# A transformer block and a linear attention block: the ramp in front of the loop re-dealt over ScalarE and VectorE

## The reference, cut to what matters

```
# block 0, for each sequence
mod = c @ ada_w.T + ada_b                     # six parts: shift, scale, gate, twice
h   = rmsnorm(x) * (1 + sc_msa) + sh_msa
q, k, v = h @ qkv_w.T                         # 16 heads of 8
q, k = rmsnorm(q), rmsnorm(k)                 # over the 8 of a head
q, k = rope3d(q, k, positions)                # sin and cos of the positions
o   = softmax(q k^T / sqrt(8)) v
x   = x + g_msa * (o @ proj_w.T + proj_b)
x   = x + g_mlp * ((silu(h2 @ w1.T) * (h2 @ w3.T)) @ w2.T)    # h2: the modulated norm of x
# block 1: layer norm, linear attention with softmax of q over 8 and of k over the tokens,
# modulated norm, silu, output projection
out = x + c * h
```

## Time and profile before

| | us |
|---|---|
| median of 3 runs | 212.56 (212.43 to 212.91) |
| the profiled execution's own time | 211.97 |
| its span, first to last instruction | 210.2 |

### The profile page before, as it was taken

How to read it: one execution, slowest core, us unless ns; L and a number is a source line. 1 busy time by engine, 2 the same in 40 slices (tenths; PEclk the granted TensorE clock), 3 DMA queues, 4 the chain that set the end, 5 groups by cost and what they waited for, 6 DMA issues and landing times.

```text
span 210.2 us, 5867 instructions
## 1 busy us (share of the span) xinstructions
PE 183.4 (87%) x1986; PEld 141.1 (67%) x1986; DVE 164.0 (78%) x488; ACT 130.7 (62%) x354; POOL 135.9 (65%) x346
## 2 busy tenths in 40 slices
PE   1796868889999999899999999999998799998742
PEld 1544556667777777777776787788886478887522
DVE  4798898897979799996666434778899589999851
ACT  1476696677777777676555784453432367999740
POOL 8889798989786867758800783167512546757642
PEclk9999999999999999999999999999999999999995
DMA  5963000000000000000000000000000000001102
GB/s 111 280 178 142 0 5 3 0 0 3 3 3 2 3 6 0 3 3 2 3 3 0 3 3 0 2 0 0 6 0 0 0 2 3 0 25 30 51 26 74
DMA packets 9915, 5.13 MB, mean 24 GB/s; under 512 B 3025, under 2 KB 9758, under 8 KB 9758
## 3 DMA queue, kind: packets, MB, share of 16 engines
q1 hardware_dynamic: 6494, 4.08, 6.4%
q10 hardware_dynamic: 3392, 0.68, 1.6%
HBM read 3.71 MB, written 1.05 MB: 23 GB/s over the span
## 4 chain that ended last, share of the span: by engine, by line
PE 61%; DVE 21%; ACT 6%; issue 6%; POOL 2%; ACTq 2%; POOLq 0%; DVEq 0%
PE bank L1769 8%; DVE qkpad L1500 8%; PE bank L1778 7%; PE bank L1860 6%; PE bank L799 5%; PE bank L810 5%; PE bank L800 5%; PE bank L786 4%; PE bank L920 3%; PE bank L1801 2%; PE bank L1837 2%; PE bank L1872 2%; PE bank L852 2%; ACT probs L1201 2%; PE bank L1830 2%
## 5 line engine op out<-in xcount | busy, mean ns | idle before, releaser
L1201 ACT ACTIVATE probs<-bank 128x512 f32<-128x512 f32 x64 | 34.7, 594 | 22.6 <-PE bank L1778 22.5
L1500 DVE TENSOR_REDUCE qkpad<-bank 128x4 f32<-128x512 f32 x64 | 41.0, 684 | 9.1 <-PE bank L1769 7.7
L1778 PE MATMUL bank<-qTm,kBD 32*128 32x128 f32 x512 | 37.1, 283 | 0.4 <-ACT probs L1201 0.4
L1769 PE MATMUL bank<-kBD,qTs 32*128 32x256 f32 x224 | 31.7, 399 | 5.7 <-DVE qkpad L1500 4.2
L1778 PEld LDWEIGHTS bank<-qTm,kBD 32*128 32x128 f32 x512 | 31.0, 186 | 1.0 <-ACT probs L1201 0.6
L1769 PEld LDWEIGHTS bank<-kBD,qTs 32*128 32x128 f32 x224 | 19.8, 184 | 10.8 <-DVE qkpad L1500 7.4
L545 ACT ACTIVATE th<-bank 128x256 f32<-128x256 f32 x24 | 9.2, 384 | 18.9 <-PE bank L800 15.5
L1860 PE MATMUL bank<-probs,vpad 128*32 128x128 f32 x512 | 18.5, 277 | 0.2
L1051 POOL TENSOR_TENSOR partner<-qk,rope 128x96 f32<-128x96 f32 x32 | 14.3, 467 | 6.7 <-ACT qk L1243 6.7
L1801 PE MATMUL bank<-ident,qkpad 128*128 128x128 f32 x96 | 16.5, 281 | 0.8 <-DVE qkpad L1598 0.8
L481 POOL TENSOR_SCALAR var<-mv 128x2 f32<-128x2 f32 x16 | 3.1, 193 | 20.3 <-DVE mv L672 18.4
(11 more groups left out here) (250 smaller groups left out, 512.3 us busy)
## 6 DMA issues: line engine op xcount, KB each, us to landing
gate<-in_cond_dram SPq DMA_DIRECT2D x1, 1024.0 KB, 4.6
out_dram<-res SPq DMA_DIRECT2D x8, 128.0 KB, 1.8
xin<-in_x_dram ACTq DMA_DIRECT2D x2, 256.0 KB, 5.1
xin<-in_x_dram SPq DMA_DIRECT2D x1, 512.0 KB, 4.9
ada_n<-in_L_cond_ada_w_dram SPq DMA_DIRECT2D x1, 256.0 KB, 5.2
w_n<-in_L_cond_w_dram SPq DMA_DIRECT2D x2, 128.0 KB
qkv_n<-in_L_cond_qkv_w_dram SPq DMA_DIRECT2D x1, 192.0 KB, 3.9
w_n<-in_L_cond_w_dram SPq DMA_DIRECT2D x1, 170.5 KB
```

What stands on the lines that cost most here:

```text
L1201: q.activation(probs[2 * r + i][:, :, :, :].rearrange("p f a t -> p (f a t)"), bank[E_BANK[i]][:, :], ACT.Exp, scale=SCALE).then_inc(s_p, 1)
L1500: q.tensor_reduce(out_, score_bank(b, r, i)[:, :].rearrange("p (f a t) -> p f a t", f=2, a=2), X_AXIS, ALU.max, negate=True).then_inc(s_ma ...
L1769: last = q.matmul(bank[S_BANK[i]][:, f * 2 * T:(f + 1) * 2 * T], qTs[b % 2][rows, f, :], kBD[b % NKB][rows, f, :, :].rearrange("p a t -> p ...
L1778: last = q.matmul(bank[E_BANK[i]][:, (2 * f + k) * T:(2 * f + k + 1) * T], kBD[t % NKB][rows, f, k, :], qTm[t % 2][rows, f, :], start=True ...
```

## The change

The head of the work is dealt anew; what is computed stays the same.

- A constant tile `warm` of 128 x 512 bf16 ones is set by VectorE as its first instruction. TensorE computes products of it, into banks that are overwritten later, in eight places of the ramp: 5, 2, 2, 1, 6, 3, 4 and 3 of them in front of waits.
- The load of sequences 4 to 7 moves from ScalarE's DMA queue to SyncE's, and the load of the rest of `ada_w` ahead of the load of sequences 8 to 15.
- The copy of the first part of `adaT` goes from VectorE to ScalarE. The squares of sequence 0 come in front of the sine.
- The sums of squares of sequences 4 to 7 are made by ScalarE with its accumulator, four rows of squares, and GpSimd adds the small constant; those of sequences 8 to 11 and 12 to 15 are made in loop steps 0 and 1, between the modulation and the second round's exponentials, and GpSimd takes the powers for four sequences at a time.
- The masks and one of the eight value tiles are set by VectorE at its start.
- Sequence 0: VectorE splits the keys and ScalarE the queries (`first_queries`), out of another bank. Sequence 2 is split by ScalarE instead of VectorE.
- The reciprocal root of sequences 4 and 5 is refined by VectorE, in seven steps right in front of the loop, instead of by GpSimd in step 0.
- On ScalarE `silu_input` comes directly behind the queries of sequence 0, and the split of sequence 1 in front of the copy of w1, the evictions of sequence 4 and the modulation of sequence 5. On TensorE the product of sequence 4 and the turning of input 5 come behind the early scores.
- Of the five small modulations behind step 0 two stay there (`V_GATE1`) and three go behind step 4.

```diff
@@ SyncE and ScalarE DMA queues
+            sp.dma_start(xin[:, HEAD_B:MID_B, :], x[HEAD_B:MID_B, :, :]...).then_inc(ld_mid, 16)
+            sp.dma_start(ada_n[:, 2:6, :], ...).then_inc(ld_ada, 16)
             sp.dma_start(xin[:, MID_B:, :], ...).then_inc(ld_x, 16)
-            sp.dma_start(ada_n[:, 2:6, :], ...).then_inc(ld_ada, 16)
...
-            input_rows(slice(HEAD_B, MID_B), ld_mid)
@@ GpSimd
+            def input_spread(rows, ready, k):
+                g.wait_ge(pv_a, ready)
+                q.tensor_scalar(ms[:, rows], ms[:, rows], 1.0, EPS0, ALU.mult, ALU.add).then_inc(p_ms, 1)
+                g.wait_ge(p_ms, k)
...
-                if not is_seq(b) or b % 2 == 0:
+                if not is_seq(b) or b % 2 == 0 or b // 2 in BY_VECTOR:      # BY_VECTOR = (0, 2)
...
-            input_rstd(slice(HEAD_B, MID_B), V_MSMID)
             turned_partner(1)
             turned_own(1)
+            input_spread(slice(HEAD_B, MID_B), A_MID, 1)
+            input_rstd(slice(HEAD_B, MID_B))
             added(1)
@@ ScalarE
             q.activation(big[:, 0:HEAD_B, :], xin[:, 0:HEAD_B, :], ACT.Square).then_inc(pv_a, 1)
+            a.wait_ge(pt, P_ADA1)
+            q.activation(adaT[:, 0:2 * D], bank[1][:, 0:2 * D], ACT.Copy).then_inc(pv_a, 1)
...
+            def square_sums_of_rows(first, sm):
+                a.wait_ge(sm, 16)
+                for b in range(first, first + HEAD_B):
                     q.activation(big[:, b, :], xin[:, b, :], ACT.Square, scale=D ** -0.5, accum_out=ms[:, b:b + 1]).then_inc(pv_a, 1)
...
+            def first_queries():
+                a.wait_ge(s_tq, 1)
+                a.wait_ge(masked, 2)
+                q.activation(qTs[0]..., bank[S_BANK[0]][:, 0:2 * T], ACT.Identity, scale=rowmask[:, 0:1]).then_inc(h_q, 1)
...
             modulated_input(1)
-            input_squares(slice(HEAD_B, MID_B), ld_mid)
+            squares(0)
             angles()
-            squares(0)
...
             input_normed(5)
+            first_queries()
+            silu_input()
             modulated_input(4)
+            keys_and_queries(1)
             weights(P_W1, ...)
             squares(4)
             queries_keys(4)
             values(4)
             modulated_input(5)
-            keys_and_queries(1)
             weights(P_W3, ...)
...
-            silu_input()
             queries_and_max(0)
+            keys_and_queries(2)
...
-            square_sums_of_rows()
...
                 modulated_input(t + 6)
+                if t < 2:
+                    square_sums_of_rows(MID_B + HEAD_B * t, ld_x)
                 exp(t, 1, 0)
@@ VectorE
+            q.memset(warm[:, :], 1.0).then_inc(warmed, 1)
             keys_seeded()
+            last_values_seeded()
+            masks()
...
             square_sums(0)
-            mean_squares(slice(HEAD_B, MID_B), A_MID, V_MSMID)
-            masks()
             square_sums(1)
             seeds(1)
-            early_rsqrt()
+            early_rsqrt(0)
...
             keys_apart(0)
-            queries(0)
             seeds(3)
...
             rowmax(1, 1, 1)
-            keys_apart(2)
-            queries(2)
             square_sums(5)
             seeds(5)
+            early_rsqrt(2)
@@ TensorE
+            def keep_warm(dst, count):
+                for _ in range(count):
+                    q.matmul(bank[dst][:, :], warm[:, 0:128], warm[:, :], start=True, stop=True)
+            e.wait_ge(warmed, 1)
+            keep_warm(W_BANK, 5)
...
+            keep_warm(W_BANK, 2)
             input_turned(0)
             input_turned(1)
             e.wait_ge(pv_a, A_QKV)
             queries_keys_values(0)
             queries_keys_values(1)
+            first_modulations()
+            keep_warm(E_BANK[1], 2)
             input_turned(2)
-            first_modulations()
             input_turned(3)
+            keep_warm(E_BANK[1], 1)
...
             prepare_hidden(w1_n)
+            keep_warm(E_BANK[1], 6)
+            queries_and_keys(0)
             input_turned(4)
-            queries_and_keys(0)
-            queries_keys_values(4)
-            input_turned(5)
+            keep_warm(E_BANK[1], 3)
             e.wait_ge(s_kq, 1)
+            e.wait_ge(h_q, 1)
             e.wait_ge(pv_v, V_MODR)
             early_scores(0, (0, 1))
             queries_and_keys(1)
+            queries_keys_values(4)
+            input_turned(5)
             e.wait_ge(pv_a, A_W1)
             prepare_hidden(w3_n)
             queries_keys_values(5)
...
             early_scores(1, (1,))
+            keep_warm(T_BANK, 4)
             queries_and_keys(2)
             e.wait_ge(s_qTm, 1)
             prepare_outputs()
+            e.wait_ge(s_v, FRONT_B)
+            keep_warm(W_BANK, 3)
```

More of the change, by code:

```diff
@@ L383, in dit_then_linear_attention, with roots_by_pool @@
         P_COND, P_ADA1, P_MOD, P_QKV, P_ADA, P_MODS, P_PAR, P_W1, P_W3, P_W2, P_BIAS, P_LIN = range(1, 13)
-        A_SQUARE, A_QKV, A_MID, A_SIN, A_ADA, A_W1, A_W3, A_TANH, A_DONE, A_SQUARES, A_OUTW = 1, 2, 3, 4, 5, 6, 7, 8, 10, 18, 19
-        V_COND, V_ADA1, V_MS, V_MOD, V_QKW, V_ANG, V_MSMID, V_MODR, V_MODS, V_LIN, V_BIAS, V_DONE = (
-            2, 3, 5, 8, 9, 18, 20, 22, 27, 31, 37, 38)
+        A_SQUARE, A_ADA1, A_QKV, A_SIN, A_ADA, A_MID, A_TANH, A_W1, A_W3, A_DONE, A_SQUARES, A_OUTW = (
+            1, 2, 3, 4, 5, 9, 10, 11, 12, 14, (18, 22), 23)
+        V_COND, V_MS, V_MOD, V_QKW, V_ANG, V_MODR, V_GATE1, V_MODS, V_LIN, V_BIAS, V_DONE = (
+            2, 4, 7, 8, 17, 19, 21, 24, 28, 34, 35)
+        BY_VECTOR = (0, 2)
+        def roots_by_pool(j):
+            return NEWT * sum(i not in BY_VECTOR for i in range(j))
         block = ctx.enter_context(nc.Block())
@@ L1002, in _, with values_seeded @@
                             pattern=[[DH, H], [0, DH]], channel_multiplier=-1).then_inc(consts, 1)
-            def values_seeded(first):
-                for k in range(first, first + NVP // 2):
+            def values_seeded(first, end):
+                for k in range(first, end):
                     q.memset(vpad[k][:, :], 0.0).then_inc(seeded_g, 1)
@@ L1011, in values_seeded, with input_rstd @@
                     q.memset(sides[:, :, :, DH:DH + 1], 1.0).then_inc(seeded_g, 1)
-            values_seeded(0)
-            def input_rstd(rows, ready):
-                g.wait_ge(pv_v, ready)
+            values_seeded(0, 3)
+            def input_rstd(rows):
                 q.tensor_tensor(rstd_x[:, rows], ms[:, rows], minus_half[:, 0:rows.stop - rows.start], ALU.pow).then_inc(p_rstd, 1)
-            input_rstd(slice(0, HEAD_B), V_MS)
+            def input_spread(rows, ready, k):
+                g.wait_ge(pv_a, ready)
+                q.tensor_scalar(ms[:, rows], ms[:, rows], 1.0, EPS0, ALU.mult, ALU.add).then_inc(p_ms, 1)
+                g.wait_ge(p_ms, k)
+            g.wait_ge(pv_v, V_MS)
+            input_rstd(slice(0, HEAD_B))
+            values_seeded(3, 4)
             g.wait_ge(pv_v, V_QKW)
@@ L1070, in rsqrt_of_heads @@
                 y_, s_, t_, w_ = ny[j % 2][:, :, :], ns[j % 2][:, :, :], nt[:, :, :], nw[:, :, :]
-                done = NEWT * (j - 1)
+                done = roots_by_pool(j)
                 g.wait_ge(s_sd, SEED * (j + 1))
@@ L1310, in _ @@
             queries_keys(1)
+            values(1)
             modulated_input(2)
-            values(1)
             modulated_input(3)
+            first_modulations()
+            square_sums_of_rows(HEAD_B, ld_mid)
             squares(2)
@@ L1394, in keys_seeded, with last_values_seeded, masks @@
                     q.memset(tile[:, 1, :, DH:DH + 1], 1.0).then_inc(seeded, 1)
+            def last_values_seeded():
+                q.memset(vpad[NVP - 1][:, :], 0.0).then_inc(seeded, 1)
+                v.wait_ge(seeded, 2 * NKB + 1)
+                sides = vpad[NVP - 1][:, :].rearrange("p (a c) -> p a c", a=2)[:, :, 0:8 * VSTEP].rearrange("p a (i c) -> p a i c", c=VSTEP)
+                q.memset(sides[:, :, :, DH:DH + 1], 1.0).then_inc(seeded, 1)
+            def masks():
+                v.wait_ge(consts, N_CONSTS)
+                q.tensor_reduce(pmask[:, :], windows[:, 0, :].rearrange("p (j a) -> p a j", a=2), X_AXIS, ALU.add).then_inc(masked, 1)
+                q.tensor_reduce(rowmask[:, :], windows[:, 1:2, :], X_AXIS, ALU.add).then_inc(masked, 1)
+                v.wait_ge(masked, 2)
+            q.memset(warm[:, :], 1.0).then_inc(warmed, 1)
             keys_seeded()
+            last_values_seeded()
+            masks()
             v.wait_ge(pt, P_COND)
@@ L1484, in centred @@
                 assert n == V_DONE
-            def masks():
-                v.wait_ge(consts, N_CONSTS)
-                q.tensor_reduce(pmask[:, :], windows[:, 0, :].rearrange("p (j a) -> p a j", a=2), X_AXIS, ALU.add).then_inc(masked, 1)
-                q.tensor_reduce(rowmask[:, :], windows[:, 1:2, :], X_AXIS, ALU.add).then_inc(masked, 1)
-                v.wait_ge(masked, 2)
             def rowmax(b, r, i):
@@ L1567, in seeds @@
```

(4 more changed lines are left out.)

86 lines of the change are left out of this document (46 added, 40 removed).

## The result

The changed kernel takes 215.32 us (median of 4 runs, 215.08 to 217.1) against 212.74 us before, runs of one session: ratio 1.015, 95% interval 1.0094 to 1.0205. It is slower by 2.6 us, where 1.1 us were forecast, and outside the range given (to 214.9). The profiled executions show 215.10 against 211.97 us and spans of 213.4 against 210.2 us, 3.2 apart. Two executions stand far outside all others (725 us of e2, 301 us of the kernel before), and nothing is read from either.

A forecast was written before the change was run, and what follows sets the result against it. The ramp's chain of handovers, mostly VectorE, was taken to bound the kernel up to step 0's second round (32.54). That round 1.4 us late, less 0.3 for gates, gave +1.1: 213.6 against 212.56 us; 8-in-10 range 211.9 to 214.9.

The forecast's parts named there:

- R0: Second round of step 0 on TensorE, at 32.54 before; forecast at 33.9, 1.4 us late.
- Start: Ramp's start: the fourth input issue leaves ScalarE's queue; normed rows at 8.15 instead of 8.35, a gain of 0.2 us.
- I take an earlier rise of the clock, around 10 us, and a sine 0.2 earlier than before: Early ramp: constant-tile products raise TensorE's clock sooner; sine bounds 0.4 us later to 0.5 earlier.
- Rival 3: Ramp: clock up only at 13 us, sine 0.3 late, root dear; 214.8 us, chance 0.09 shared with another rival.
- ScalarE's queue in front of the scores of sequence 1: Early scores to sequence 1's scores: ScalarE's reordered work uses up all 2.1 us gained; scores at 24.5 against 24.46.
- The second root on VectorE: In front of step 0: seven root products added on VectorE, 2.35 us; row maxima of sequence 2 at 32.6, not 31.21.
- Gates, root off POOL and row sums: Steps 0 and 1: fewer modulations gain 0.3 us; POOL losing the root and the moved row squares count 0.
- The products: Constant-tile products on TensorE: able to help before 12 us, worth nothing behind 14 us, where the clock is already up.
- The circle: Loop behind 32.54: a fixed circle of scores, row maxima, second round; a delay is neither grown nor recovered.

The follow-up runs named there:

- e2: The changed kernel with no product of the constant tile, the tile still set: 217.40 us.
- e7: The kernel before with 15 products of the constant tile added in front of TensorE's waits in its last steps: 210.84 us, ratio 0.9921.
- e8: The kernel before with one memset of 128 x 2048 on VectorE in front of the row maxima of sequence 2: 216.59 us.
- e1: The changed kernel with the sine again in front of the squares of sequence 0 on ScalarE: 215.09 us.
- e4: The changed kernel with the first half of sequence 1's scores in front of the w1T wait and the product of sequence 5 on TensorE: 216.06 us.
- e5: The changed kernel with sine first, second root on GpSimd and first half of sequence 1's scores earlier, all together: 212.04 us, ratio 0.9977.
- e3: The changed kernel with the second root (sequences 4 and 5) back on GpSimd: 213.87 us, ratio 1.0060.
- e2b: The changed kernel with no product of the constant tile, run once more for a trace: 216.84 us.

## Why the prediction was wrong

The direction and the place were right, the size was not: +1.1 forecast, +2.6 measured. R0 was forecast at 33.9 and came at 35.13, 1.2 later; 0.2 more than forecast was won back in steps 1 and 2; and the end, which the sum left out, took 0.5 by the medians and 1.1 in the profiled pair.

*Start.* Right in kind, and partly by luck: VectorE has the modulation at 6.44, where the prediction kept 7.1, and the normed rows at 7.85 where 8.15 was forecast. TensorE found its first operands at 3.75 for 4.54; but e7 and e8, which have the old start, found them at 3.91 and 3.33, so the loads scatter by as much.

*The step that failed first: "I take an earlier rise of the clock, around 10 us, and a sine 0.2 earlier than before".* The clock rose at 13.0 us, the product of sequence 0 still ran at 0.85 us a pass, and the sine was 0.6 later than before, at 11.88, where 11.1 was taken. VectorE's seeds, taken for 13.2, started at 13.84; by e1 that is less the sine than the products of sequences 0 and 1 at the low clock, since the squares of sequence 1 hold VectorE even with an early sine. The prediction had let these squares come as early as VectorE was free. With seeds of 1.87 us instead of 1.1 (the long ones at 0.65, next to POOL's rotations) and a root of 2.64 for 3.0, the early scores came at 20.41 against a forecast of 19.3. These 1.1 us went through to R0: from the early scores to those of sequence 1 it took 5.32 (forecast 5.2), from there to R0 9.40 (forecast 9.4). Rival 3 had the late clock and the late sine, with a chance too small, and a root dearer than it was.

*ScalarE's queue in front of the scores of sequence 1.* Right, shown by e4 and e5: 5.3 us with the order of the change, 3.03 without it, as in the kernel before.

*The second root on VectorE.* Right: 2.27 us for a forecast of 2.35, of which e3 finds 1.6 on the path. Its products took 0.41 and 0.50 us while POOL rotated and 0.22 once it waited, as the earlier trace rows had it. TensorE's first round, taken as ready at 29.8, started at 31.00, behind ScalarE's split of sequence 2, and is what e3 runs into.

*Gates, root off POOL and row sums.* The sum of 0.5 for 0.3 is half luck. Step 1, where the gates stood, gives 0.19. The other 0.34 are step 2's seeds beside a less busy GpSimd, where the prediction put GpSimd's lighter load at nothing; that it is the moved root is not shown, as e3, with the root back on GpSimd, has the same step 2. The row sums cost nothing that can be seen.

*The products: "Behind 14 us the clock is already up and they can give nothing".* Wrong. e2b shows the clock falling there without them; they are worth 1.5 to 2.1 us in this kernel and hide a part of its cost. The trace of before could not show it, since its clock did not fall there in that execution; in e8's, with the same ramp, it did. (The Trainium skill, TensorE: Matmul & The Clock Gate, HAM oscillation, describes this: idle gaps between bursts put the array back to the low clock. I had weighed that page's rule only for the rise. e2b, e4 and e8's second fall agree, with 2.06 us for early scores of 1.15, and half steps of 4.7 for 3.2; e8's first fall, behind a wait of 0.76 us, is not explained by it.)

*The circle "in which a delay is neither grown nor recovered".* True of the loop, 2.06 throughout from step 2 on, and false of the end: in the profiled pair the fall caught the changed kernel with four pairs of output products to go and the one before with two, which is 0.66 us. That pair compares a usual execution with one of the few in which the kernel before has its fall late, so in the medians little of this is left; there the sum misses the 0.48 whose cause is open.

## What to carry to other kernels

A gain upstream is worth what is left of it at the next handover: follow every engine's list from there to the point that releases the loop, and look what was put in front of the instruction that others wait for. A wait on TensorE costs its length and sometimes more, because products behind a gap can run at half the clock, as e4 and e8 show; count its gaps in the changed order, in the ramp and at the end, and try a few idle products in the last waits early on (here 1.8 us for fifteen). Where a kernel's runs spread, compare their mean granted clock before comparing their traces, and ask whether the profiled execution is a usual one.

## What the runs showed of the hardware that was not expected

- The fall at the end came at 204.7 and 204.2 us in two kernels whose work was 2 us apart there, in the opposite order, and between 199.5 and 207.0 us in the other kernels without tail products. How much work it catches differs between executions of one kernel: those of the kernel before differ by some 0.7 us with it.
- A memset of 1.76 us on VectorE made a kernel 4.0 us slower.
- In e8 the clock rose at 15.9 us and fell again at 19.3, although TensorE had idled only 0.76 us since 14.7.
- Fifteen products of ones in the last waits made a tuned kernel 0.8% faster.
- Before the rise the profile gives the granted clock as 1.00; only the durations (0.85 for 0.49 us a pass) tell that it is low.
